# Expert stage of a convolution, attention and expert-mixture block: third layer in four 64x64 tiles over two banks, gates brought by DMA, loops written out, weights loaded beside the last image

## What is computed

```
x = x + conv3x3(group_norm(x), sign(W_conv))
t = tokens(x)                                   # (32, 3136, 64)
t = t + attention(layer_norm(t)) + layer_norm(t)
u = layer_norm(t)                               # "x2"
feat = mean(u, axis=0)                          # over the 32 images: (3136, 64)
w = softmax(feat @ Wr + br)                     # gates: one row of 8 for each of the 3136 positions
h = relu(bn1(u @ W1[e] + b1[e]))                # e = 0..7, all 64 wide
h = relu(bn2(h @ W2[e] + b2[e]))
out = t + sum_e w[:, e] * (h @ Wo[e] + bo[e])
```

## Time and profile before

| | |
|---|---|
| median of three runs | 7242.83 us |
| the profiled execution, its own time | 7243.7 us |
| its span in the trace | 7241.9 us |
| attention block | 0 to about 5931 us |
| parameters, gates and first prologue | 5931 to 5999 us |
| units | 5999 to 7236 us |
| busy share over the span: TensorE, VectorE, ScalarE, POOL | 96%, 69%, 60%, 76% |

### The profile page before, as it was taken

How to read it: one execution, slowest core, us unless ns; L and a number is a source line. 1 busy time by engine, 2 the same in 40 slices (tenths; PEclk the granted TensorE clock), 3 DMA queues, 4 the chain that set the end, 5 groups by cost and what they waited for, 6 DMA issues and landing times. The chain is left out here.

```text
span 7241.9 us, 132870 instructions
## 1 busy us (share of the span) xinstructions
PE 6983.8 (96%) x48626; PEld 3566.1 (49%) x48626; DVE 5012.9 (69%) x9053; ACT 4372.2 (60%) x9329; POOL 5473.8 (76%) x5524
## 2 busy tenths in 40 slices
PE   7999999999999999999999999999999959999999
PEld 4555555555555555555555555555555523333332
DVE  6777777777777777777777777777777714444444
ACT  1666666666666666666666666666666634555555
POOL 2888888888888888888888888888888852222222
PEclk7999999999999999999999999999999979999999
DMA  1011111111111111111111111111111003333333
GB/s 30 15 23 23 23 23 23 23 24 23 23 23 23 23 24 23 23 23 23 23 23 23 23 23 23 23 23 23 23 24 23 10 25 78 80 82 83 84 83 79
DMA packets 324411, 240.54 MB, mean 33 GB/s; under 512 B 253368, under 2 KB 307000, under 8 KB 319808
## 3 DMA queue, kind: packets, MB, share of 16 engines
q1 hardware_dynamic: 311616, 208.17, 12.9%
q0 software_dynamic: 12288, 25.71, 1.6%
HBM read 156.30 MB, written 77.48 MB: 32 GB/s over the span
## 5 line engine op out<-in xcount | busy, mean ns | idle before, releaser
L611 ACT ACTIVATE probs<-bank 128x392 f32<-128x392 f32 x6400 | 2797.0, 496 | 1887.1 <-PE bank L658 1849.9
L478 DVE TENSOR_REDUCE part_max<-bank 128x1 f32<-128x448 f32 x5600 | 3211.6, 613 | 583.6 <-PE bank L651 574.6
L651 PE MATMUL bank<-ks,qs 96*128 96x448 f32 x5600 | 2347.4, 424 | 55.4 <-DVE part_max L478 50.0
L425 POOL TENSOR_TENSOR psum<-psum,probs 128x392 f32<-128x392 f32 x2048 | 2100.4, 1026 | 320.5 <-ACT probs L611 34.0
L422 POOL TENSOR_TENSOR psum<-probs 128x392 f32<-128x392 f32 x2048 | 2100.6, 1026 | 236.7 <-ACT probs L611 224.4
L658 PE MATMUL bank<-qs,ks 97*128 97x392 f32 x6400 | 2026.3, 367 | 15.2 <-ACT probs L611 12.8
L667 PE MATMUL bank<-probs,vs 128*32 128x392 f32 x12288 | 1765.4, 506 | 37.2 <-POOL psum L425 28.1
L669 PE MATMUL bank<-psum,ones 128*32 128x392 f32 x4096 | 1737.8, 506 | 0.0
L651 PEld LDWEIGHTS bank<-ks,qs 96*128 96x128 f32 x5600 | 1065.5, 190 | 1230.4 <-DVE part_max L478 746.0
L658 PEld LDWEIGHTS bank<-qs,ks 97*128 97x128 f32 x6400 | 1190.9, 190 | 405.5 <-ACT probs L611 222.3
L1007 DVE SCALAR_TENSOR_TENSOR h<-ebank,tmp_n,gate_w 128x784 f32<-128x784 f32 x512 | 529.2, 1034 | 644.2 <-PE ebank L1060 644.2
(11 more groups left out here) (127 smaller groups left out, 5336.1 us busy)
## 6 DMA issues: line engine op xcount, KB each, us to landing
xin<-in_x_dram SPq DMA_DIRECT2D x64, 784.0 KB, 8.9
xs<-x_dram SPq DMA_DIRECT2D x512, 98.0 KB, 2.4
xpk<-in_x_dram SPq DMA_DIRECT2D x64, 392.0 KB, 12.7
t_dram<-t SPq DMA_DIRECT2D x32, 784.0 KB, 5.1
x_dram<-xn SPq DMA_DIRECT2D x32, 784.0 KB, 6.6
res<-t_dram SPq DMA_DIRECT2D x256, 98.0 KB, 2.5
out_dram<-fin POOLq DMA_DIRECT2D x256, 98.0 KB, 2.5
row_dram<-row_max SPq DMA_DIRECT2D x192, 2.0 KB
```

The costliest lines, as they stand in the source:

```text
L425: add = gp.tensor_tensor(into, into, three, ALU.add)
L478: v.tensor_reduce(part_max[:, b, m:m + 1], m_bank[place.bank()][:, 0:MW], AX.X, ALU.max).then_inc(m_used, 1)
L611: s.activation(probs[:, held(c, k), :], s_bank[n % 3][:, 0:2 * QW], ACT.Exp, scale=SCALE).then_inc(p_ready, 1)
L651: mm(m_bank[place.bank()][:, 0:MW], qs[par][0:KS, b * P:(b + 1) * P], ks[par][0:KS, m * MW:(m + 1) * MW], start=True, stop=True).then_inc( ...
```

## The change

- Parameters go into `xin` (class `Parameters`), loaded by SP right after the stores of image 30, while image 31 is in its attention; `zero`, `roots` and `fold` are set into the steps of image 31 on VectorE and ScalarE. `select` is gone.
- The logits alternate between the two row halves and go to two banks. The turned gates are written to HBM (`gate_dram`) and read back as `gate_w`, spread over 64 partitions each, by two DMAs for each piece (`load_gates`), into two buffers. The bias of all eight pieces is computed once before the units.
- Blocks 2 and 3 are one block; the 512 units are written out in straight code, with constants in the waits, and there is no drain between groups or pieces.
- Layer 1 writes three single banks in turn, not two pairs. ScalarE signals after each of its two operations.
- Layer 3 becomes four tiles of 64x64: rows 0 to 63 (even expert) into `even_bank[p]`, rows 64 to 127 into the one `odd_bank`. VectorE adds them one after the other (`first_half` after the first unit of the next pair, `second_half` after the second).
- SP waits in one fixed order for each pair; at the first pair of pieces 1 to 6 it also waits for `h2_ready` and issues the gates of the next piece before that pair's `res`.
- POOL alternates: bias of pair q, then store of pair q-1.

```diff
@@ -378,6 +377,10 @@
+                        if n == images - 2:
+                            sp.wait_ge(pad_hi, images * CH)
+                            sp.wait_ge(pad_lo, images * CH)
+                            experts.load(sp)
...
@@ -532,6 +535,10 @@
+                        if c == QC - 3 and im.c == images - 1:
+                            experts.zero(dve)
+                        if c == QC - 1 and im.c == images - 1:
+                            experts.fold(dve)
                         dve.wait_ge(proj_done, im.count(QC, c + 1))
...
@@ -611,6 +618,8 @@
+                        if c == QC - 2 and im.c == images - 1:
+                            experts.roots(act)
                         act.wait_ge(o_done, im.count(QC, c + 1))
...
+class Parameters:
...
+    def load(self, sp):
+        def load(dst, src):
+            sp.dma_start(dst, src).then_inc(self.loaded, 16)
+        for h in range(2):
+            rows = slice(h * C, (h + 1) * C)
+            load(self.w1f[rows], self.w1.rearrange("e d h -> d e h"))
+            load(self.w2f[rows], self.w2.rearrange("e h k -> h e k"))
+            load(self.wr_sb[rows], self.w_r)
+            load(self.w3f[rows], rows_of(self.w3)[h])
...
+    def roots(self, act):
+        s, tmp, cols = self.nc.scalar, self.tmp, self.cols
+        act.wait_ge(self.loaded, self.LOADS)
+        act.wait_ge(self.zeroed, 2)
+        s.activation(tmp["l1"], cols["v1"], ACT.Ln, bias=self.eps3)
+        s.activation(tmp["l2"], cols["v2"], ACT.Ln, bias=self.eps3)
+        s.activation(self.s2row, self.s2row, ACT.Ln, bias=self.eps3).then_inc(self.logs_ready, 1)
+        act.wait_ge(self.logs_ready, 1)
+        s.activation(tmp["r1"], tmp["l1"], ACT.Exp, scale=-0.5)
+        s.activation(tmp["r2"], tmp["l2"], ACT.Exp, scale=-0.5)
+        s.activation(self.s2row, self.s2row, ACT.Exp, scale=-0.5).then_inc(self.powers_ready, 1)
+
+    def zero(self, dve):
+        v = self.nc.vector
+        dve.wait_ge(self.loaded, self.LOADS)
+        v.memset(self.c2_st, 0.0).then_inc(self.zeroed, 1)
+        v.memset(self.eps3, 1e-3).then_inc(self.zeroed, 1)
...
+        dve.wait_ge(self.zeroed, 2)
+        dve.wait_ge(self.powers_ready, 1)
...
+        v.tensor_scalar(tmp["n2"], tmp["c2"], -1.0, None, ALU.mult)
+        link(v.tensor_tensor(self.s2row, self.s2row, self.g2row, ALU.mult))
+        v.tensor_tensor(self.w2f, self.w2f, self.s2row.rearrange("p (e m) -> p e m", e=EXP), ALU.mult)
...
+        last.then_inc(self.ready, 1)
+
+
+class Unit:
+
+
+    def __init__(self, n, groups):
+        self.n = n
+        self.e, self.pair = n % EP, n // EP
+        self.p = self.pair % 2
+        self.piece, self.at = self.pair // (2 * groups), self.pair % (2 * groups) * 2
+        self.half, self.r = self.piece // CH, self.piece % CH
...
+        gate_w = sb("gate_w", [P, 2, EP, CW])
+        bias_w = sb("bias_w", [P, 2 * CH, CW])
+        xs = sb("xs", [P, 2, 2, CW])
...
+        l1_bank = [ctx.enter_context(nc.psum_tensor(f"l1_bank{j}", [P, 512], F32)) for j in range(3)]
+        l2_bank = ctx.enter_context(nc.psum_tensor("l2_bank", [P, 2, 512], F32))
+        even_bank = [ctx.enter_context(nc.psum_tensor(f"even_bank{j}", [P, 512], F32)) for j in range(2)]
+        odd_bank = ctx.enter_context(nc.psum_tensor("odd_bank", [P, 512], F32))
...
+        def load_pair(sp, q):
+            for j in range(2):
+                sp.dma_start(xs[0:C, q.p, j, :], part(x2_dram, q, j)).then_inc(xs_loaded[q.p], 16)
+                sp.dma_start(xs[C:P, q.p, j, :], part(x2_dram, q, j ^ 1)).then_inc(xs_loaded[q.p], 16)
...
+        def load_gates(sp, piece):
+            at = piece // CH * RW + piece % CH * CW
+            for a in range(2):
+                src = gate_dram.rearrange("(e a) n -> a e n", a=2)[a, :, at:at + CW]
+                sp.dma_start(gate_w[a * HID:(a + 1) * HID, piece % 2, :, :], src.partition_broadcast(HID)).then_inc(gates_loaded[piece % 2], 16)
...
+        def store(gp, q):
+            gp.wait_ge(fin_ready[q.p], q.pair // 2 + 1)
+            for h in range(2):
+                dst = out_rows[q.at + h, q.half, :, q.r * CP:(q.r + 1) * CP, :]
+                gp.dma_start(dst, fin[h * C:(h + 1) * C, q.p, :].rearrange("c (r w) -> c r w", w=HW)).then_inc(stored[q.p], 16)
...
+                for q in pairs[0:2]:
+                    load_pair(sp, q)
+                    load_res(sp, q)
+                for n in range(TURNS):
+                    sp.wait_ge(turn_saved, n + 1)
+                    sp.dma_start(gate_dram[:, turn_cols(n)], gates_t[:, turn_cols(n)]).then_inc(gates_stored, 16)
+                    for piece in range(2):
+                        if turns_for(piece) == n + 1:
+                            sp.wait_ge(gates_stored, 16 * n + 16)
+                            load_gates(sp, piece)
+                sp.wait_ge(gates_stored, 16 * TURNS)
+                for q in pairs[1:]:
+                    before = pairs[(q.n // EP) - 1]
+                    if q.n // EP >= 2:
+                        sp.wait_ge(xs_used[q.p], q.pair // 2)
+                        load_pair(sp, q)
+                    if q.pair % per_piece == 0 and q.piece + 1 < 2 * CH:
+                        sp.wait_ge(h2_ready, q.n)
+                        load_gates(sp, q.piece + 1)
+                    if q.n // EP >= 2:
+                        sp.wait_ge(fin_ready[q.p], q.pair // 2)
+                        load_res(sp, q)
...
+                for q in pairs:
+                    gp.wait_ge(res_loaded[q.p], 32 * (q.pair // 2 + 1))
+                    gp.wait_ge(bias_saved, q.piece + 1)
+                    gp.tensor_tensor(res[:, q.p, :], res[:, q.p, :], bias_w[:, q.piece, :], ALU.add).then_inc(res_ready[q.p], 1)
+                    if q.pair:
+                        store(gp, pairs[q.pair - 1])
+                store(gp, pairs[-1])
...
+                for n in range(2 * CH):
+                    act.wait_ge(bias_done, n + 1)
+                    s.activation(bias_w[:, n, :], l1_bank[n % 3][:, 0:CW], ACT.Copy).then_inc(bias_saved, 1)
+                for u in units:
+                    act.wait_ge(l1_done, u.n + 1)
+                    for j in range(2):
+                        at = j * EP + u.e
+                        s.activation(h1[:, u.n % 2, j, :], l1_bank[(2 * u.n + j) % 3][:, 0:CW], ACT.Relu,
+                                     bias=tmp["c1"][:, at:at + 1], scale=tmp["s1"][:, at:at + 1]).then_inc(h1_ready, 1)
...
+                def first_half(q):
+                    dve.wait_ge(l3_done[q.p], q.pair // 2 + 1)
+                    dve.wait_ge(res_ready[q.p], q.pair // 2 + 1)
+                    v.tensor_tensor(res[:, q.p, :], odd_bank[:, 0:CW], res[:, q.p, :], ALU.add).then_inc(odd_used[q.p], 1)
+
+                def second_half(q):
+                    dve.wait_ge(odd_used[q.p], q.pair // 2 + 1)
+                    if q.pair >= 2:
+                        dve.wait_ge(stored[q.p], 32 * (q.pair // 2))
+                    v.tensor_tensor(fin[:, q.p, :], even_bank[q.p][:, 0:CW], res[:, q.p, :], ALU.add).then_inc(fin_ready[q.p], 1)
...
+                    if u.n % (EP * per_piece) == 0:
+                        dve.wait_ge(gates_loaded[u.piece % 2], 32 * (u.piece // 2 + 1))
+                    dve.wait_ge(l2_done, u.n + 1)
+                    v.scalar_tensor_tensor(h2[:, u.n % 2, :, :], l2_bank[:, :, 0:CW], tmp["n2"][:, u.e:u.e + 1],
+                                           gate_w[:, u.piece % 2, u.e:u.e + 1, :].broadcast_to([P, 2, CW]), ALU.max, ALU.mult).then_inc(h2_ready, 1)
+                    if u.pair and u.e == 0:
+                        first_half(pairs[u.pair - 1])
+                    if u.pair and u.e == 1:
+                        second_half(pairs[u.pair - 1])
...
+                for b in range(RB):
+                    for h in range(2):
+                        rows = slice(h * C, (h + 1) * C)
+                        last = mm(l2_bank[:, h, b * EXP:(b + 1) * EXP], feat[rows, b * P:(b + 1) * P], par.wr_sb[rows], start=True, stop=True)
...
+                pe.wait_ge(b3_ready, 1)
+                for n in range(2 * CH):
+                    at = n // CH * RW + n % CH * CW
+                    pe.wait_ge(turn_saved, turns_for(n))
+                    if n >= 3:
+                        pe.wait_ge(bias_saved, n - 2)
+                    mm(l1_bank[n % 3][:, 0:CW], b3w[:].rearrange("e a c -> e (a c)"), gates_t[:, at:at + CW], start=True, stop=True).then_inc(bias_done, 1)
+                pe.wait_ge(bias_saved, 2 * CH)
+                def layer1(u):
+                    if u.e == 0:
+                        pe.wait_ge(xs_loaded[u.p], 64 * (u.pair // 2 + 1))
+                    if u.n:
+                        pe.wait_ge(h1_ready, 2 * u.n - 1)
...
+                        bank = l1_bank[(2 * u.n + half) % 3]
+                        for out_rows_, of, side in ((rows, u.e * 2, 0), (slice(C - half * C, P - half * C), u.e * 2 + 1, 1)):
```

(23 more changed lines are left out.)

358 lines of the change are left out of this document (113 added, 245 removed).

## The result

The changed kernel takes 7054.98 us in the median of four runs (7053.75 to 7055.79), the kernel before 7244.61 in the same comparison: ratio 0.9739 with a 95% interval of 0.9722 to 0.9756. The profiled execution has 7055.03 us and a span of 7053.2. The forecast was 7037 (range 7005 to 7115): right in sign and in its main mechanism, and 18 us too low. The largest error is one term, the stalls at the changes of piece, 23 us too cheap; a third of it is hidden by the units, which came out 8 us shorter than forecast.

A forecast was written before the change was run, and what follows sets the result against it. TensorE was taken to bound the units, with 0.31 us each streaming nothing. Gains 111.9 + 60.3 - 7 + 41.3 - 0.6 = 205.9 us off 7243.7 gave 7037.8, so 7037 for the median, range 7005 to 7115.

The forecast's parts named there:

- Units: In the 512 units: each falls from 2.292 to 2.07 us, bound by the loop over layer 2's bank; gain 111.9 us.
- The 0.31 beside layer 3: In each unit: 0.31 us in which TensorE streams nothing, beside the layer with another tile shape; expected to go.
- the 0.16 of waits: Before layer 2's weight load: register arithmetic of two waits, 0.16 us off the drain's 2.23, leaving 2.07.
- Rival (a): In the units: the gap belongs to layer 3's place, not tile shape; unit stays 2.29, total 7150; chance 7%.
- Rival (b): In the units: TensorE alone bounds, the bank loop being shorter than read; total 6991; chance 8%.
- Rival (d): In the units: straight code cannot be fetched fast enough; unit 3.1 us, total 7585; chance 3%.
- Changes of piece: Between pieces: drain, five matmuls, copies and refill go, each of seven falling from 10.68 to 2.07 us; gain 60.3 us.
- SP at the changes of piece: At pieces 1 to 6: SP's wait and queued issues make xs late; 1.2 us each, -7 us in all.
- Rival (c): At pieces 1 to 6: the gates hold xs back by 10 us six times; total 7097; chance 12%.
- Before the first unit: From setup to first gate operation: parameter loads, roots and folds leave, logits shorten; sum -41.3 us.
- Last image: In image 31's attention: the inserted loads, roots and folds overrun by 0 us, at most 4.2.
- Tail: At the kernel's end: one more VectorE addition, +0.6 us.

The follow-up runs named there:

- e1_l3_128: The changed kernel with layer 3 back in two 128x64 tiles, one bank and one VectorE addition: 7161.39 us.
- e2_gate_half: The changed kernel with VectorE's gate operation on half of the columns, the other half of h2 staying zero: 7008.73 us.
- e7b_drains: The version with spread gates, but TensorE finishes layers 2 and 3 of the last two units before starting each of pieces 1 to 7: 7040.56 us.
- version with spread gates: The changed kernel with each next piece's gates as eight DMAs of 98 KB in eight pairs, without SP's wait: 7024.65 us, ratio 0.9698 to the kernel before.
- e4_gates_small: The changed kernel, same order and wait of SP, but gate DMAs of pieces 2 to 7 carry 8 of 392 columns: 7032.51 us.

## Why the prediction was right, and where it missed

- **Units.** Right in place and nearly in size. The 0.31 beside layer 3 went with the tile shape, the bank loop took over, and the 0.16 of waits that I took off the old drain's 2.23 are real. 2.055 against 2.07: 511 x 0.015 = 7.7 us on the good side. Rival (a) is excluded by `e1_l3_128`, in which layer 3 keeps its place and the gaps come back with the shape. Rival (b) is excluded here and shown to be the next floor by `e2_gate_half`. Rival (d) is excluded: of the waits of matmuls in the units, 19.7 us end with `xs` and 0.8 with VectorE, none with anything else, at 48 instructions in 2.05 us.
- **Changes of piece.** 60.3 gained, as summed: a change of piece is a step like any other (2.05 us against 10.68). `e7b_drains` shows 21 of it as drain.
- **SP at the changes of piece: the step that failed.** Its mechanism, its six places and its order of issues were as written. The price was 1.2 each, bounds 0 and 3; it was 5.0. I had timed `xs` behind the gates with the 2.4 us that it takes in a quiet stretch, although 784 KB had just been issued ahead of it; the row of 392 KB in 12.7 us was there, and I kept it out of the bound. And I priced the wait alone, not the half clock that followed all six waits (1.5 each). Rival (c) had the mechanism, at double the price.
- **Before the first unit.** The steps measured: 38.2 for the moved ones (37 forecast), 5.72 for the logits (6), 8.47 for the turns (8.5), 7.9 from the first bias matmul to the first unit (8.8). These came early enough to make up for the last image's 1.7, and the first unit started within 0.2 of the forecast. The step mis-sized here is the last one, from the first unit to the first gate operation: 3.4 forecast, 5964.20 - 5958.78 = 5.42 measured, and that is the 2.2 by which the first gate operation came late. The forecast had reckoned with half clock for a part of the stretch only; it held for all of it (the first window below, where the kernel before has 0.59 over its 4.11 us, the second). And the second unit's layer 1 waited 0.80 for ScalarE (the last line), where the kernel before starts both without a wait (the x16 in the earlier trace rows).

```profile
5958.78:5964.20 5.42, 4.62 (x28) 1.55 (x32) 0.00 (x1) 2.49 (x4) 0.00 (x0) 0.50 0.02 3
5999.23:6003.34 4.11, 3.96 (x29) 1.44 (x32) 0.00 (x1) 2.90 (x5) 1.08 (x2) 0.59 0.49 133
```

```profile
5961.16 1.59 PE L1079 MATMUL l_bank<-xs,xin 64*64 64x392 f32 x8 [0.80 <-ACT h L985]
```

- **Last image.** 0 forecast, 1.7 measured, inside the bound of 4.2.
- **Tail.** +0.6 forecast, +0.2 measured.

So the total came nearer than its terms: 23 us too little for the stalls stand against 8 too much for the units. That they offset each other is luck; the range would have held the result without it (7063).

The version with spread gates (7024.65) beats both kernels.

## What to carry to other kernels

When one limit of a loop is lifted, look for the next one in a place where the first is absent: the drain of the old kernel showed the bank loop, down to the waits inside it. In such a loop every instruction between the signal and the first use counts, so the last wait should be against a constant and sit on the instruction that needs it. Put a bulk transfer between loads of a pipeline in slices, and price one by what it does to the loads queued behind it and to the clock after the stall, not by the wait alone.

## What the runs showed of the hardware

- A register addition cost TensorE nothing ahead of a wait (unit 2.13 with or without it) and about 0.1 us when it carried the wait (2.226); a waiting instruction of its own between signal and weights cost 0.08 us (2.13 instead of 2.05).
- Two gate DMAs of 392 KB (5.2 us to landing in the median) took the DMA share over the stall from 0.42 to 0.82 and held the `xs` load behind them to 3.5 us from the end of its issue, against 1.9 with small gates.
- After TensorE's wait of 1.3 us in `e4_gates_small` the granted clock stayed at 1.00, that is 2.4 GHz; after the 3.19 us in the changed kernel it was 0.50, 1.2 GHz, for 3.3 us. Waits of like length went either way in other runs (3.03 us: 1.00; 2.35 us: 0.50).
- Matmuls of 64 rows took 5.72 us for 26 on alternate halves, 10.43 one half after the other, both at half clock.
